# Delta rule: two unread two-byte products behind each group of small products

## What is computed

```python
x = x + _L0_attn_ref(_layernorm(x, axis=-1), ...)
x = x + _L0_ffn_ref(_layernorm(x, axis=-1), ...)
...
x = x + _L2_attn_ref(_layernorm(x, axis=-1), ...)
```

```python
A = jnp.where(tri, 0.0, -jnp.einsum('bhncd,bhned->bhnce', kb, k))
for i in range(1, chunk):
    upd = jnp.einsum('...k,...kj->...j', A[..., i, :], A[..., :, :i])
    A = A.at[..., i, :i].add(upd)
inv = A + jnp.eye(chunk, dtype=A.dtype)
u = inv @ v
w = inv @ kb
...
    u_adj = ui - wi @ S
    out_i = qi @ S + attn @ u_adj
    S = S + jnp.swapaxes(ki, -1, -2) @ u_adj
```

## Time and profile before

| | us |
|---|---|
| median of 3 executions | 6494.34 |
| lowest, highest | 6486.61, 6507.39 |
| the profiled execution, whole | 6507.19 |
| its span, first to last instruction | 6505.9 |
| PE busy | 4478.3 |
| DVE busy | 3330.1 |
| stretches of the small levels in layer 0 | 39 to 52 each, 8 of them |
| stretches of the small levels in layer 2 | 32 to 35 each, 8 of them |

### The profile page before, as it was taken

One profiled execution on the slowest core, in us unless ns is written; L12 is line 12 of the kernel. 1 busy time (PEld: TensorE's weight loads), 2 busy tenths in 40 slices (PEclk: granted clock), 3 DMA queues, 4 the chain that ended last, 5 costly groups with the idle time before them and its releaser, 6 DMA issues.

```text
span 6505.9 us, 103238 instructions
## 1 busy us (share of the span) xinstructions
PE 4478.3 (69%) x43660; PEld 3358.1 (52%) x43660; DVE 3330.1 (51%) x8382; ACT 1948.3 (30%) x4164; POOL 1066.8 (16%) x784
## 2 busy tenths in 40 slices
PE   3756565655888888883655656657777787777388
PEld 3545444444655556552544545445544555546377
DVE  7575767524444444447255464554454444544423
ACT  2222222221333333230233232324443344433122
POOL 3030303032011111001600000010111101110334
PEclk6555555567888888785766566668888888888599
DMA  9000000032000000001300000000000000000155
GB/s 252 1 1 1 1 1 1 1 115 75 1 1 1 1 1 1 1 1 32 61 1 1 2 1 2 2 2 1 1 1 1 1 1 1 1 1 1 56 145 142
DMA packets 140751, 148.69 MB, mean 23 GB/s; under 512 B 7792, under 2 KB 127986, under 8 KB 139776
## 3 DMA queue, kind: packets, MB, share of 16 engines
q1 hardware_dynamic: 118880, 124.04, 6.6%
q0 software_dynamic: 21408, 18.05, 1.6%
HBM read 83.21 MB, written 59.76 MB: 22 GB/s over the span
## 4 chain that ended last, share of the span: by engine, by line
PE 50%; DVE 33%; ACT 8%; issue 4%; POOL 2%; DMA 1%; another core or an unknown queue 1%; SPq 0%; DVEq 0%; POOLq 0%; ACTq 0%
DVE weights L1210 3%; PE banks_lane L420 3%; PE banks_lane L3088 3%; PE banks_lane L3059 2%; DVE work L1210 2%; PE banks_lane L3574 2%; PE banks_lane L2992 2%; PE banks_lane L1819 2%; PE banks_lane L3076 2%; ACT work L3153 2%; PE banks_lane L3063 2%; PE banks_lane L3041 2%; PE banks_lane L1805 1%; PE banks_lane L933 1%; PE banks_lane L1804 1%
## 5 line engine op out<-in xcount | busy, mean ns | idle before, releaser
L420 PE MATMUL banks_lane<-constants,work 128*128 128x128 f32 x920 | 190.4, 355 | 412.9 <-DVE work L406 159.8
L420 PE MATMUL banks_lane<-constants,weights 128*128 128x128 f32 x612 | 128.0, 352 | 449.9 <-DVE weights L406 142.1
L400 POOL TENSOR_TENSOR weights<-weights,constants 128x4 f32<-128x4 f32 x80 | 82.7, 1033 | 1945.4 <-DVE weights L395 1945.4
L420 PEld LDWEIGHTS banks_lane<-constants,work 128*128 128x128 f32 x920 | 146.2, 185 | 478.6 <-DVE work L406 135.8
L420 PEld LDWEIGHTS banks_lane<-constants,weights 128*128 128x128 f32 x612 | 93.6, 181 | 475.8 <-issue 192.7
L3153 ACT ACTIVATE work<-banks_lane,weights 128x192 f32<-128x192 f32 (+1 forms) x512 | 248.0, 495 | 290.1 <-DVE weights L3235 290.1
L400 POOL TENSOR_TENSOR work<-work,constants 128x4 f32<-128x4 f32 x72 | 73.3, 1018 | 1274.7 <-DVE work L395 1274.7
L3243 POOL TENSOR_TENSOR weights<-weights,constants 128x16 f32<-128x16 f32 x64 | 185.3, 2896 | 527.5 <-DVE weights L3166 527.5
L3231 DVE TENSOR_REDUCE weights<-banks_lane 128x2 f32<-128x384 f32 (+1 forms) x256 | 122.4, 520 | 257.2 <-PE banks_lane L3063 257.2
L3088 PE MATMUL banks_lane<-work 128*128 128x64 f32 x1792 | 232.8, 287 | 9.1 <-ACT work L3114 9.1
L3088 PEld LDWEIGHTS banks_lane<-work 128*128 128x128 f32 x1792 | 224.1, 204 | 18.4 <-ACT work L3114 12.0
(11 more groups left out here) (809 smaller groups left out, 11774.5 us busy)
## 6 DMA issues: line engine op xcount, KB each, us to landing
work<-experts_dram_l_ffn SPq DMA_DIRECT2D x39, 964.0 KB
room_l_ffn<-work SPq DMA_DIRECT2D x30, 1188.0 KB, 14.0
work<-experts_dram_l_ffn SPq DMA_DIRECT2D x23, 512.0 KB
weights<-weights_dram SPq DMA_DIRECT2D x1, 4833.5 KB, 14.6
work<-room_l_ffn SPq DMA_DIRECT2D x36, 132.0 KB, 3.2
weights<-weights_dram SPq DMA_DIRECT2D x1, 4112.0 KB, 12.3
weights<-room_l_ffn SPq DMA_DIRECT2D x26, 132.0 KB, 4.3
weights<-weights_dram SPq DMA_DIRECT2D x1, 3378.0 KB, 11.1
```

The source lines that it names most:

```text
L400: pool.tensor_tensor(n.rstd, n.rstd, c("neghalf", cols=(0, n.rstd.shape[1])), ALU.pow).then_inc(*u.pool.step(name))
L420: done = pe.transpose(bank[0:rows, t * P:(t + 1) * P], block, c("ident"))
```

## The change

Behind each left and each right group of the four small levels, and behind the semaphore step that reports the group, TensorE runs two further products: the bfloat16 identity times the bfloat16 mask `later` of 512 columns, written to bank 1 of the same lane. Each of them raises the lane's TensorE semaphore by one. No engine waits for either, and nothing reads bank 1 before `values_pe` starts it anew. To reach the masks, `Delta` and the two lane classes are handed `run` or `run.masks`.

```diff
+    def unread_pe(self, pe, u):
+
+        for _ in range(2):
+            pe.matmul(u.banks[1][:, :], self.masks("ident"), self.masks("later")).then_inc(*u.pe.step())
+
     def levels_pe(self, pe, u, pair):
         b = u.banks
         for n in range(1, SMALL_LEVELS):
...
             made.then_inc(*u.pe.step(f"left{pair}_{n}"))
+            self.unread_pe(pe, u)
             yield f"left{pair}_{n}"
             pe.wait_ge(*u.dve.at(f"part{pair}_{n}"))
...
             made.then_inc(*u.pe.step(f"right{pair}_{n}"))
+            self.unread_pe(pe, u)
             yield f"right{pair}_{n}"
...
-    def __init__(self, c, arena):
-        self.norm, self.delta = Norm(arena), Delta(c, arena, DK, False)
+    def __init__(self, run, arena):
+        c = run.c
+        self.norm, self.delta = Norm(arena), Delta(c, run.masks, arena, DK, False)
```

More of the change, by code:

```diff
@@ L746, with __init__ @@
 class Delta:
-    def __init__(self, c, arena, dv, scaled):
-        self.c, self.dv, self.width = c, dv, HEADS * dv
+    def __init__(self, c, masks, arena, dv, scaled):
+        self.c, self.masks, self.dv, self.width = c, masks, dv, HEADS * dv
         self.NT, self.AT, self.X, self.XT, self.T1 = (arena.take(2, HEADS, P) for _ in range(5))
@@ L990, in __init__ @@
         self.run, self.c, self.w, self.X = run, run.c, w, X
-        self.lanes = [L0AttnLane(run.c, arena) for _ in range(LANES)]
+        self.lanes = [L0AttnLane(run, arena) for _ in range(LANES)]
         self.low, self.one_more, self.rest, self.temp_inv = (arena.take(1) for _ in range(4))
@@ L2482, with __init__ @@
 class L2AttnLane:
-    def __init__(self, c, arena):
-        self.norm, self.delta = Norm(arena), Delta(c, arena, L2_ATTN_DV, True)
+    def __init__(self, run, arena):
+        c = run.c
+        self.norm, self.delta = Norm(arena), Delta(c, run.masks, arena, L2_ATTN_DV, True)
         self.before = [arena.take(L2_ATTN_CONV - 1 + SEQ) for _ in range(2)]
@@ L2506, in __init__ @@
         self.rate = arena.take(HEADS)
-        self.lanes = [L2AttnLane(run.c, arena) for _ in range(LANES)]
+        self.lanes = [L2AttnLane(run, arena) for _ in range(LANES)]
     def start_act(self, act, u):
```

## The result

The changed kernel took 6535.3 us (median of 12 runs, 6510.0 to 6555.5) against 6496.8 us for the kernel before in the same series. The ratio is 1.005, with a 95% interval of 1.0036 to 1.0064: 0.5% slower, some 32 us (23 to 42); the two medians lie 38.6 us apart. The forecast was +27 us, 6521 us.

What follows compares the result with a forecast made beforehand. VectorE was taken to bound layer 0's small levels and TensorE's instruction fetch layer 2's. Layer 0's 8 us plus layer 2's 19 us (2.4 us, 8 times) gave +27 us, 6521 us against the median, range 6492 to 6560.

Steps and rivals of the forecast that it cites:

- (c): Layer 2's levels: 256 instructions with products take 3.6 us, below the 3.96 us fetch, so products fill stops at no cost.
- Layer 0: Only the couple between lane 0's first left group and lane 1's scores costs: 1.0 us, 8 us over 8 pair instances.
- (a): Layer 2, ahead of lane 1's scores, where VectorE idles: one couple in the open, 1.0 us per instance, 0.55 as lower bound.
- (b): Layer 2's levels: 14 groups with four more instructions each, 56 at 3.96 / 256 us, cost 0.87 us per instance.
- high bound: Drain paid ahead of couples too and VectorE's results late: 4.3 us per block of 256, 46 us in all.
- (d): Layer 2, end of the small levels: half of the last unread couple counts, 0.5 us per instance.
- Rival 1: Unread products lift the clock through the levels and speed up the products behind them in layer 2: 6473 us, chance 0.12.
- Rival 3: Fetch stops under the products, so layer 2 pays each couple in full: 136 us with layer 0, 6630 us, chance 0.08.
- rival 2: No change that can be told: more is hidden than counted, 5 to 18 us, say 6506 us, chance 0.22.

Runs made afterwards that it cites:

- not_first: The changed kernel without the two unread products behind each left group of level 1; 1.0022 of the kernel before.
- half: The kernel before with every second product of the small levels left out in layer 2, inverse not right; 6406.4 us against a median of 6497.0, one run.
- narrow2: The changed kernel with its two unread products per group 8 columns wide instead of 512; 1.003 of the kernel before.
- l0_only: The changed kernel with the unread products in layer 0 alone, none in layer 2; 1.0008 of the kernel before.
- first8: The kernel before plus eight unread products of 512 columns behind each lane's left group of level 1, none elsewhere; 1.0073 of the kernel before.
- narrow8: The changed kernel with eight unread products of 8 columns behind each group in place of two of 512; 1.0071 of the kernel before.
- last8: The kernel before plus eight unread products behind each lane's last right group of the small levels, none elsewhere; 1.0033 of the kernel before.

## Why the prediction was right, point by point

**The bounds of the two stages held.** VectorE in layer 0: 14 of 16 couples cost 0.1 us over all eight instances (not_first). The fetch of instructions in layer 2: half of them is half of the time (half), and products without width cost about what the whole ones cost (narrow2). That the fetch goes on while TensorE works, which step (c) had to assume, is seen in the packets: each starts after a stop's end.

**Layer 0, 8 us forecast, 5 to 6 us measured.** The place and the price are right: 0.96 to 1.01 us in each instance of l0_only, VectorE's idle time 2.13 to 2.25 us where 2.2 was forecast. In after some instances paid less at the open place (0.10 to 1.02 us). The couple took 0.96 us in all eight; the scores behind it ran partly at the upper clock (1.82 to 2.06 us in seven, 2.11 before). In the instance that paid 0.10, VectorE's own work in the stretch was 0.8 us shorter, and why was not looked into. And about 0.4 us each came back in the levels of three or four of the eight, which had not been counted.

**Layer 2, 19 us forecast, 22.5 measured (25 against the mean of three traces), by terms that partly cancel.** (a) The open place was forecast at 1.0 us each, 8 in all; it was 3.5. The couple there takes 0.54 us in three instances, as this row of the chain of after shows, 0.77 to 0.80 in four and 0.96 in one:

```profile
3958.90 0.54 PE banks_lane L786 x2
```

The instance that I read was also the slowest of the eight in before: VectorE's idle time ahead of L2797 is 0.99 us there, 0.04 to 0.65 in the others, and the sum rose from 3.2 to 7.1 us in after. I had 0.55 as the lower bound and chose the upper value from the mean clock of the whole stretch; the clock of the place itself was to be looked for. (b) The 56 instructions were put at 0.87 us, 7 in all; narrow2 shows 13 for them alone, with some 5 us of scatter. The principle is right (a fixed time for 256 instructions). The price of one block, 3.96 us, was read from one of the two slowest of the eight stretches (3.52 to 3.97 us); their mean is 3.74. Most of the rest lies in where the last stop falls: five stops more, not 1.75. This is the term that was sized wrong, at 7 us for 13 to 16. (c) That the products' own time costs nothing in the levels holds for the sum (+14.6 with it, +13.0 without their width), but not at every place: products at the start of lane 1's levels are on the path (first8), and my step covered them with a stop that is not due yet. It is a close thing behind that place too: a group and its couple take 0.98 + 0.96 = 1.94 us at the lower clock, 1.94 x 1.94 = 3.8 us for 256 instructions, where I had 3.6 from a group of 0.86. A group behind a full-width couple takes 0.98 to 1.01 us; the 0.86 was one behind another small group. 3.8 is as long as the fetch, and without the clock's rise the high bound (4.3 for a block) would have been nearer. (d) The last couple was put at half, 4 us in all. The tail is 4.3 us longer in after and 2.3 shorter in narrow2, so that the couples' width costs up to 6.6 there.

**Sum: 27 us forecast, 27 in the trace, 32 (23 to 42) by the ratio.** The agreement of the total is better than that of its terms, and in part luck: layer 0 was too high by 3 us, (a) by 4.5, and (b) too low by 6 or more.

**The clock** was to stay at 0.50 to 0.6 and in after, from lane 1's first transpose to its last, it was 0.54 to 0.60 in the eight stretches of layer 0 and 0.62 to 0.90 in those of layer 2, where it had been 0.50 in all sixteen. It is the width that lifts it: in narrow2 it stays at 0.50. Rival 1 had its premise, that the full-width products lift it, and failed at the condition that I had named: it must hold to the products behind. There the row of after reads 0.50, and so do the other seven tails of layer 2. **Rival 3** is out by the stops, which came down from 79 us over the eight stretches of layer 2 to 36, and by the sum: 2.8 us for an instance of layer 2 and not 16. The Trainium skill ("Runtime: NRT & Kernel Launch", section "Instruction fetch mechanics") calls crossing into the next block mostly hidden. Here it is not, for groups of small products: 101 us went when half of the instructions did. Of **rival 2** the ratio's interval leaves nothing, since it starts at 1.0036.

**What stays open:** how much of narrow2's +13.0 us is where the blocks' borders fall (56 instructions an instance account for 7) and why narrow8 costs only 1.7 times that; how the +14.6 us of after divides between instructions and the couple at lane 1's start (narrow2 gives +13.0 to the first, not_first 11.5 to the second or to three blocks of the fetch); and what decides which of the three distances a block takes.

## What to carry to other kernels

A stop named "issue" with no releaser, at an equal distance each time, in a run of very short instructions, was the fetch of instructions here. It can be told by the packets of the instruction queue: one ended shortly ahead of each stop's end. There, work on the same engine costs by the blocks of instructions that it adds, and its own length is covered until it fills the stop. Where another engine sets the pace, look for the one place at which the added work stands ahead of something that this engine waits for in order; that place is the price. And read the clock at the place of the cost, not over the stretch.

## What the runs showed of the hardware that was not expected

- A few full-width bfloat16 products between small ones raise the granted clock: 0.50 to 0.63 in a stretch of layer 0's levels (10.99 us more of TensorE's work in 40), 0.90 with four products a group in layer 2. As many products of 8 columns don't (0.50 in narrow2, in narrow8 too). One stop of 1.21 us was followed by a return to the lower level (a couple of 0.54 us at 3976.20, of 0.96 us at 3983.28).
- The clock can return to the lower level and stay there for 16 us while TensorE is busy 15.96 of them, with 1.50 us of idle time in the 7 us before, 0.76 at most at a time (last8).
- The fetch of 256 TensorE instructions takes one of three times here in nearly all cases, 3.47, 3.75 or 4.02 us, with or without the change.
- TensorE goes on 1.19 to 1.60 us after the packet of 16 KB has ended, and the next packet starts only 1.04 to 1.90 us after that: in these stops one block was fetched at a time (251 stops in five traces).
